# Pieces of the first loads, the order of the first DMAs, self-attention two slots later and 64-column products in a perceiver layer

## What is computed

```
# cross-attention, 16 heads of 32 columns
q = layernorm(x) @ Wq.T + bq ; k = ctx @ Wk.T + bk ; v = ctx @ Wv.T + bv
s = where(z >= 0, z + 1, 1 / (1 - z)),  z = q k^T / sqrt(32)
x = x + (s / sum(s) @ v) @ Wo.T + bo
# self-attention, 8 heads of 64 columns that share one K and one V
y = layernorm(x) ; x = x + softmax(mask(q k^T / sqrt(512))) v @ Wp + bp
# mixture: 2 shared experts, and the best 2 of 8 by gates = xf @ rW + rb
x = x + mean(shared experts) + sum(w_e * expert_e)
```

## Time and profile before

| | us |
|---|---|
| median of 3 runs | 1284.3 (1282.82 to 1285.09) |
| profiled execution | 1284.68 |
| its span on the core | 1283.0 |
| PE busy | 1265.1 |
| DVE busy | 648.8 |
| ACT busy | 634.0 |
| POOL busy | 437.6 |

### The profile page before, as it was taken

One profiled execution on the slowest core, in us unless ns is written; L12 is line 12 of the kernel. 1 busy time (PEld: TensorE's weight loads), 2 busy tenths in 40 slices (PEclk: granted clock), 3 DMA queues, 4 the chain that ended last, 5 costly groups with the idle time before them and its releaser, 6 DMA issues.

```text
span 1283.0 us, 29915 instructions
## 1 busy us (share of the span) xinstructions
PE 1265.1 (99%) x13126; PEld 1098.9 (86%) x13126; DVE 648.8 (51%) x936; ACT 634.0 (49%) x1085; POOL 437.6 (34%) x203
## 2 busy tenths in 40 slices
PE   8999999999999999999999999999999999999998
PEld 8888888888788888788888878798989999999997
DVE  5343353443363363463453354756776555565555
ACT  3545554454545544545544536646545444554443
POOL 2345345544555545645456535200022000100000
PEclk9999999999999999999999999999999999999999
DMA  6121011012011003012003111674556499999990
GB/s 216 72 89 67 18 55 39 33 42 92 19 63 67 18 22 133 18 59 71 18 22 115 67 50 49 232 294 164 173 190 205 154 335 359 354 347 337 356 402 36
DMA packets 32775, 174.89 MB, mean 136 GB/s; under 512 B 5944, under 2 KB 8152, under 8 KB 14464
## 3 DMA queue, kind: packets, MB, share of 16 engines
q1 hardware_dynamic: 30896, 168.16, 35.6%
q0 software_dynamic: 1744, 4.76, 1.1%
HBM read 166.84 MB, written 6.06 MB: 135 GB/s over the span
## 4 chain that ended last, share of the span: by engine, by line
PE 87%; POOL 3%; DMA 3%; issue 2%; DVE 2%; ACT 2%; SPq 0%; DVEq 0%; POOLq 0%; ACTq 0%
PE bank L728 20%; PE bank L740 18%; PE bank L1079 11%; PE sc L1096 8%; PE sc L756 7%; PE sc L941 6%; PE bank L960 3%; PE bank L769 3%; PE sc L960 3%; DMA wqt<-in_aq 2%; POOL xn L587 2%; PE bank L833 1%; DMA wqt<-in_wq 1%; POOL xa L599 1%; ACT tt L1208 1%
## 5 line engine op out<-in xcount | busy, mean ns | idle before, releaser
L587 POOL TENSOR_TENSOR xn<-xn,tt 128x1024 f32<-128x1024 f32 x96 | 230.2, 2398 | 339.3 <-DVE tt L1325 338.3
L1208 ACT ACTIVATE tt<-sc 128x512 f32<-128x512 f32 (+1 forms) x208 | 107.8, 603 | 360.3 <-PE sc L756 360.2
L1423 DVE TENSOR_TENSOR wsl<-ring,wsh 128x2048 fp32r<-128x2048 f32 x72 | 166.8, 2316 | 111.6 <-ACT wsh L1163 111.1
L1312 DVE TENSOR_SCALAR kk<-bank,bkt 128x512 f32<-128x512 f32 (+2 forms) x130 | 80.8, 622 | 232.4 <-PE bank L728 232.2
L728 PE MATMUL bank<-cxh,wkh 128*128 128x512 f32 (+2 forms) x512 | 181.4, 354 | 1.5 <-DVE va L1320 1.0
L728 PE MATMUL bank<-cxl,wkh 128*128 128x512 f32 (+2 forms) x512 | 174.7, 341 | 0.0
L728 PE MATMUL bank<-cxh,wkl 128*128 128x512 f32 (+2 forms) x512 | 174.2, 340 | 0.0
L740 PE MATMUL bank<-wvh,cxh 128*128 128x512 f32 (+1 forms) x416 | 163.6, 393 | 0.0
L740 PE MATMUL bank<-wvl,cxh 128*128 128x512 f32 (+1 forms) x416 | 162.9, 391 | 0.0
L740 PE MATMUL bank<-wvh,cxl 128*128 128x512 f32 (+1 forms) x416 | 162.3, 390 | 0.0
L1163 ACT CAST wsh<-ring 128x2048 fp32r<-128x2048 f32 x72 | 137.4, 1908 | 48.2 <-PE sc L1096 20.9
(11 more groups left out here) (270 smaller groups left out, 2027.9 us busy)
## 6 DMA issues: line engine op xcount, KB each, us to landing
ring<-in_w SPq DMA_DIRECT2D x112, 1024.0 KB, 7.0
ctxt<-in_ctx SPq DMA_DIRECT2D x15, 1024.0 KB, 4.9
ctxt<-in_ctx SPq DMA_DIRECT2D x8, 642.0 KB, 3.9
ctxt<-in_ctx SPq DMA_DIRECT2D x10, 512.0 KB, 3.5
wqt<-in_wo SPq DMA_DIRECT2D x4, 1024.0 KB, 4.9
wqt<-in_aq SPq DMA_DIRECT2D x4, 1024.0 KB, 8.4
wqt<-in_ap_ SPq DMA_DIRECT2D x4, 1024.0 KB, 7.0
yrows<-K SPq DMA_DIRECT2D x1, 2048.0 KB, 9.2
```

Source lines behind the costliest of these rows:

```text
L587: e.tensor_tensor(dacc[0:kn, y, :], dacc[0:kn, y, :], tt[0:kn, w, :], ALU.add).then_inc(s["da_pool"], 1)
L1208: e.activation(weights_view(m, kn, hb), score_read(m, kn, hb), ACT.Relu, scale=-1.0).then_inc(s["t_act"], 1)
L1423: e.tensor_tensor(wsl[m % 3][:], ring[slot(unit_split(m))][:], wsh[m % 3][:].bitcast(F32), ALU.subtract).then_inc(s["wl_dve"], 1)
```

## The change

- wk and the first context rows are loaded, split and used in four pieces each (one per 128 rows of the contraction) instead of two and one; x is loaded in two.
- wq is loaded ahead of wv.
- `slot_of` has 8 for 6: every self-attention step of tiles 0 to 2 is two slots later (only the gate of tile 2 stays). The second split of `wqt` is at step 6 instead of 5. The first, five slots ahead of step 0, moves with it.
- The gate and the self-attention values are computed in halves of 64 rows, and the values have 64 columns instead of 128 (the other 64 were a copy that nobody read).

```
-    return next((t for t in range(3) if slot == (slot_of(t, 0) - 5, slot_of(t, 5))[what]), None)
+    return next((t for t in range(3) if slot == (slot_of(t, 0) - 5, slot_of(t, 6))[what]), None)
...
-    return 2 * PER * t + 2 * PER + 6 + (9 if d == 10 else d)
+    return 2 * PER * t + 2 * PER + 8 + (9 if d == 10 else d)
...
-            e.dma_start(wkt[:, 0:2, :], wk[:, 0:2, :]).then_inc(s["wk_in"], 16)
-            load_ctx(0)
-            e.dma_start(wkt[:, 2:4, :], wk[:, 2:4, :]).then_inc(s["wk2_in"], 16)
+            for c in range(4):
+                e.dma_start(wkt[:, c, :], wk[:, c, :]).then_inc(s[f"wk{c}_in"], 16)
+                e.dma_start(ctxt[:, 256 * c:256 * c + 256], ctx0[0, :, 256 * c:256 * c + 256]).then_inc(s[f"cx{c}_in"], 16)
             e.dma_start(bkt[:], bk).then_inc(s["bk_in"], 16)
-            e.dma_start(xres[:], x).then_inc(s["x_in"], 16)
+            e.dma_start(xres[:, 0:2, :], x[:, 0:2, :]).then_inc(s["x_in"], 16)
+            e.dma_start(xres[:, 2:4, :], x[:, 2:4, :]).then_inc(s["x2_in"], 16)
+            e.dma_start(wqt[:], wq).then_inc(s["wq_in"], 16)
             e.dma_start(wvt[:], wv).then_inc(s["wv_in"], 16)
-            e.dma_start(wqt[:], wq).then_inc(s["wq_in"], 16)
...
+                for c in range(4):
                     for x_, (a, b) in enumerate(((0, 0), (1, 0), (0, 1))):
+                        if x_ == 0:
+                            e.wait_ge(s["wkh_act"], c + 1)
+                            e.wait_ge(s["cx_act"], c + 1)
                         elif x_ == 1:
+                            e.wait_ge(s["wkl_dve"], c + 1)
+                        else:
+                            e.wait_ge(s["cl_dve"], c + 1)
...
                 for c in range(4):
-                    m = e.matmul(dst[:, 0:8], xaT[:, c, :], rwt[:, c, :], start=(c == 0), stop=(c == 3))
+                    for h in range(2):
+                        r = slice(64 * h, 64 * h + 64)
+                        m = e.matmul(dst[r, 0:8], xaT[:, c, r], rwt[:, c, :], start=(c == 0), stop=(c == 3))
...
                 for c in range(4):
-                    m = e.matmul(dst[:, P:2 * P], xaT[:, c, :], avt[:, c, :], start=(c == 0), stop=(c == 3))
+                    for h in range(2):
+                        r = slice(64 * h, 64 * h + 64)
+                        m = e.matmul(dst[r, P:P + 64], xaT[:, c, r], avt[:, c, 0:64], start=(c == 0), stop=(c == 3))
...
-                e.tensor_copy(V2[:], src[:, P:2 * P]).then_inc(s["proj_read"], 1)
+                e.tensor_copy(V2[:, 0:64], src[:, P:P + 64]).then_inc(s["proj_read"], 1)
```

More of the change, by code:

```diff
@@ L699, in first_keys @@
                 n = width(0)
-                for h in range(2):
+                for c in range(4):
                     for x_, (a, b) in enumerate(((0, 0), (1, 0), (0, 1))):
[L702 to L706, removed]
+                        if x_ == 0:
+                            e.wait_ge(s["wkh_act"], c + 1)
+                            e.wait_ge(s["cx_act"], c + 1)
                         elif x_ == 1:
-                            e.wait_ge(s["wkl_dve"], h + 1)
-                        elif h == 0:
-                            e.wait_ge(s["cl_dve"], 1)
+                            e.wait_ge(s["wkl_dve"], c + 1)
+                        else:
+                            e.wait_ge(s["cl_dve"], c + 1)
                         for g in range(4):
[L712 to L716, removed]
+                            m = e.matmul(key_bank(0, g)[:, 0:n], (wkh, wkl)[a][:, c, g * P:(g + 1) * P],
+                                         (cxh, cxl)[b][:, 0, c, 0:n], start=(x_ == 0 and c == 0),
+                                         stop=(x_ == 2 and c == 3))
+                            if (c, x_) == (3, 2):
                                 m.then_inc(s["k_pe"], 1)
@@ L723, in keys @@
                 if g == 0:
-                    e.wait_ge(s["ch_act"], i + 1)
+                    e.wait_ge(s["ch_act"], i)
                     e.wait_ge(s["cl_pool"], i)
@@ L1176, in act @@
             e.preload_act_table_set("natural_log_exp_and_others")
-            e.wait_ge(s["wk_in"], 16)
-            e.copy(wkh[:, 0:2, :], wkt[:, 0:2, :]).then_inc(s["wkh_act"], 1)
-            context_hi(0)
-            e.wait_ge(s["wk2_in"], 16)
-            e.copy(wkh[:, 2:4, :], wkt[:, 2:4, :]).then_inc(s["wkh_act"], 1)
+            src, hi, lo = ctx_views(0)
+            for c in range(4):
+                e.wait_ge(s[f"wk{c}_in"], 16)
+                e.copy(wkh[:, c, :], wkt[:, c, :]).then_inc(s["wkh_act"], 1)
+                e.wait_ge(s[f"cx{c}_in"], 16)
+                e.copy(hi[:, c, :], src[:, c, :]).then_inc(s["cx_act"], 1)
             e.wait_ge(s["eps_dve"], 1)
@@ L1474, in vector @@
             src, hi, lo = ctx_views(0)
-            for c in range(2):
+            for c in range(4):
                 e.wait_ge(s["wkh_act"], c + 1)
-                e.tensor_tensor(wkl[:, 2 * c:2 * c + 2, :], wkt[:, 2 * c:2 * c + 2, :],
-                                wkh[:, 2 * c:2 * c + 2, :].bitcast(F32), ALU.subtract).then_inc(s["wkl_dve"], 1)
-                if c == 0:
-                    e.wait_ge(s["ch_act"], 1)
-                    e.tensor_tensor(lo, src, hi.bitcast(F32), ALU.subtract).then_inc(s["cl_dve"], 1)
-            e.wait_ge(s["x_in"], 16)
+                e.tensor_tensor(wkl[:, c, :], wkt[:, c, :], wkh[:, c, :].bitcast(F32),
+                                ALU.subtract).then_inc(s["wkl_dve"], 1)
+                e.wait_ge(s["cx_act"], c + 1)
+                e.tensor_tensor(lo[:, c, :], src[:, c, :], hi[:, c, :].bitcast(F32), ALU.subtract).then_inc(s["cl_dve"], 1)
             for h in range(2):
+                e.wait_ge(s[("x_in", "x2_in")[h]], 16)
                 for t in range(2 * h, 2 * h + 2):
```

10 lines of the change are left out of this document (5 added, 5 removed).

## The result

The changed kernel took **1299.2 us** (median of 4 runs, 1298.7 to 1300.0) beside 1283.6 for the kernel before on the same chip (4 runs, 1282.7 to 1285.1): a ratio of 1.0121, 95% interval 1.0103 to 1.0138. It is slower by 15.6 us. The forecast was 1294 us, with a range of 1288 to 1300.

The account below looks back on a forecast made before the run. TensorE was taken as the bound, busy 1265.1 of 1283.0 us, leaving 18 us of waits to win. Terms summed to +10.1 us: 1284.7 + 10.1 - 0.4 = 1294.4, given as 1294 us, range 1288 to 1300.

Parts of the forecast that it names:

- start: wq ahead, and its clock: First queries: wq landing earlier cuts PE's wait by 1.8 us; without a clock fall there, 1.8 us more.
- start: the pieces: First loads: pieces let the first keys start without a 0.3 us wait; given 0 as a separate gain.
- columns: Self-attention values in 64 columns: 0.3 us won per tile, -1.2 us for four; nothing counted for the gate.
- shift: aq, xa, third turn: Self-attention two slots later: PE's waits for aq (-3.7) and xa (-2.0) go, the third turn waits longer (+1.5 us).
- (2) attended products: Attended products moved from slot 41 to 43: PE waits for DVE's copy of the values, +3.2 us.
- (3) the three stalls: Slots 29-30, 55-56, 81-82: wol behind POOL's sum holds DVE, so PE's values wait 4.4 us three times, +13.2 us.
- (4) clock at them: After each 4.4 us PE gap the clock may fall, 1.8 us each; half of three falls taken, +2.7 us.
- Rival A: Slots 29, 55, 81: DVE gets its steps in around POOL's instructions, no stalls or clock falls; 1278.5 us, 10%.
- Rival C: The clock falls in all three gaps at PE's values, 5.4 us on top of 7.4; 1297.1 us, 20%.
- B: The three stalls at PE's values come but the clock stays up; 1291.7 us, 27%.
- rival D: The start wins nothing: pieces land late or the clock still falls there, 3.6 us more; 1298.0 us, 5%.

Follow-up runs that it names:

- fastest kernel: Kernel before plus two-slot shift, first output-weight split at slots 27, 53, 79, attended products at slot 44, 64-column products, wq ahead of wv, no pieces: 1276.9 us.
- slot 43: The fastest kernel with the attended products back at slot 43, where the change puts them, instead of 44: 1278.9 us, ratio 0.9960.
- stall put back: The fastest kernel with only the first split of the output weights back behind the sums of slots 29, 55 and 81: 1295.8 us, ratio 1.0091.
- the run with quarters: The changed kernel with wol made on POOL by four instructions of 512 columns instead of one of 2048, same place: 1293.4 us, ratio 1.0075.
- the split moved back: The changed kernel with only the first split of the output weights (wol, woh) back in slots 27, 53 and 79: 1279.9 us, ratio 0.9963.

## Why the forecast held, and where it was short

Each step of the prediction beside what the pairs of runs gave, by differences of medians:

| Step | forecast | measured | from |
|---|---|---|---|
| start: wq ahead, and its clock | -3.6 | -2.7 | wq alone against before |
| start: the pieces | 0 | +2.1 (+2.3) | with and without them |
| columns | -1.2 | -1.4 | wq and columns against wq |
| shift: aq, xa, third turn | -4.2 | -2.8 | fastest kernel against wq and columns |
| (2) attended products | +3.2 | +2.0 | slot 43 against 44 |
| (3) the three stalls | +13.2 | +12.4 | PE's waits, stall put back |
| (4) clock at them | +2.7 | +6.5 | the rest of 18.9 |
| sum | +10.1 | +16.1 | the change measured +15.6 |

**What held.** Step (3), the largest, came out as worked: the position of `wol` in POOL's queue, DVE kept out until 0.1 us behind its end, DVE's queue late by 4.4 and PE's values waiting 4.16 to 4.2 us, at the three places named. The sign and most of the size rest on it. That the range held owes something to luck: the start and the shift gave 4.4 us less than forecast and the clock cost 3.8 more, while the attended products, the columns and the stalls cost 2.2 less. Rival A, that DVE gets its steps in between, is refuted by the 4.48 us of L1465, and the run with quarters shows that what DVE waits for is the end of a single instruction. The three gains of waits (aq, xa, wq) are all in the trace of after.

**Step (4) was mis-sized.** I took half of three falls of 1.8 us. The clock fell at every one of the three gaps, in the changed kernel and in two others with gaps of 4.2 us, and in part for 6.8 us instead of 3.4: 6.5 us. Rival C had the number of falls right and their length not. The argument for B, that full work runs up to each gap, did not protect the clock. The Trainium skill (TensorE: Matmul & The Clock Gate, section "HAM oscillation — how this bites in real kernels") says that every burst behind such a wait starts cold; the gaps of 4.2 us agree, nine of nine in the three traces; at those of 2.85 us the clock fell once in three. By that rule and falls of 1.8 us the forecast would have been rival C's 1297.1.

**Step (2) had the right place and the wrong cost.** The waits are 0.9 us, not 1.45. I had 2.3 us from the start of the scores to the end of the first half and 3.7 to the end of DVE's copy. In tile 0 of the changed kernel the scores start at 361.36, and these are 2.6 and 3.4 us:

```profile
363.31 0.65 PE L875 MATMUL bank<-xaT,V 64*64 64x256 f32 x4
364.86 0.87 PE L875 MATMUL bank<-xaT,V 64*64 64x256 f32 x4 [0.90 <-DVE va L1323]
```

The first half takes 0.65 us, and I had allowed 0.3. The waits are free in themselves as far as the runs tell, and yet cost 2.0 us, because the clock falls behind them: in the changed kernel twice. I had not thought of a fall behind a gap shorter than the 2.2 us of the one I had seen. Rival C and my sum both lacked these.

**The start was wrong in one step**: x is issued 2.4 us later, behind the pieces (at 5.06, not 2.69), and the forecast gave that no cost. The step beside it, "they can begin when the warm-up ends", held: the first keys begin at 7.13 us instead of 7.63. But the transposes need the normalised x, and DVE starts on x 2.8 us later than before (13.29, not 10.47). I costed six more DMAs as 0.45 us of issue each and took their bytes to arrive as before; from 4 to 8 us they arrive at 253 instead of 405 GB/s. How much of x's delay is the later issue and how much the lower rate stays open. The 0.8 us that I gave as a bound, for pieces that land slower, is about what the traces show for the whole start, 32.19 against 33.00, but I kept 1.8 for the wait and 1.8 more for the clock; rival D named it with 5%. The gain of the clock at the start (1.8) is real, and belongs to wq: it comes without the pieces, with less scatter, and with them it is not certain: with the wait cut to 0.8 us I expected no fall, and the queries of 5.38 us stand behind a wait of 0.77.

**The shift's gain** is 2.8 and not 4.2. PE's waits of these two kernels differ by as little: 2.6 for aq and 2.7 for xa at both turns go, and 2.0 at the third turn and 0.6 at the attended products come or stay, 2.7 us. The aq wait of 3.7 in the earlier trace rows was already 2.6 there, in two waits instead of three: the third, 1.2 us in tile 2 of the kernel before, is one of 0.9 us put down to DVE's copy `va` with wq ahead alone, and is not there with the columns too. So a part of what the table gives to the columns may be this wait; the runs do not separate them.

## What to carry to other kernels

Before an instruction of GpSimd is moved, look at what DVE does while it runs, and at the instruction that it now follows: two back to back kept a small cast of DVE waiting for the whole of the second (4.48 us). The long one was cheaper in quarters (1293.4 us, not 1299.2) and cheapest in a slot in which DVE normalises nothing (1279.9). A wait of TensorE can cost its length and the clock with it, in this kernel half as much again for gaps of 4.2 us, and by my reading 1.5 us at each fall behind a gap of 0.9; so a step is best placed by the profile's waits and the granted clock together. Do not cut a first load into small DMAs for an earlier start without reading the GB/s of that stretch: cutting 512 KB into 256 and 128 KB cost more than the overlap gave, and swapping two whole loads gave the entire gain.

## What the runs showed that I had not expected

- The granted clock falls at gaps as short as 0.88 to 0.91 us, and not each time: at both in three profiles (the changed kernel, the shift alone, the quarters), at one of two in two others (the split moved back, slot 43). The work ahead of them is 64 small products of 32x64 and the first half of the attended products, in which PE counts as busy. At the start of the kernel with the split moved back it fell behind gaps of 1.38 and 0.77 us with eight transposes between them; the changed kernel has the same gaps and no fall there.
- A fall lasts 3.4 us or 6.8, nothing between, in all 23 falls ahead of the last microseconds in the fourteen traces here. The twelve that begin after PE has resumed last 3.4, the eight that begin 0.3 us or more before it resumes last 6.8. Of the three that begin 0.16 us or less before, one is long. At equal gaps of 4.2 us the fall began from 2.3 us before PE resumed (675.8, gap until 678.0) to 0.7 after (471.0, gap until 470.3), so the price of one stall varies, and only a mean over several is worth forecasting.
- From 4 to 8 us the DMA engines at a share of 1.02 moved 253 GB/s with loads of 128 and 256 KB cut by partitions, and at 1.01 386 GB/s with loads of 512 KB and more, with rows of at least 4 KB in both. The cause is open.
